# A decoder kernel's first batch: operand rows placed in two groups of eight heads, small loads behind the first, new order and bank tables

## The reference, cut to what matters

```python
x = _layernorm(x + _L0_attn_ref(x, ...))         # causal self-attention, 16 heads of 8, q and k normed
x = _layernorm(x + _L0_xattn_ref(x, ctx, ctx, ...))  # cross-attention, 16 heads of 8
x = _layernorm(x + _L0_ffn_ref(x, ...))          # 8 gated experts
x = _layernorm(x + _L1_attn_ref(x, ...))         # linear attention in chunks of 128
x = _layernorm(x + _L1_xattn_ref(x, ctx, ...))   # cross-attention, 8 heads of 128
x = _layernorm(x + _L1_ffn_ref(x, ...))          # gated feed-forward, 384 wide
```

## Time and profile before

| | us |
|---|---|
| median of 3 runs | 483.26 |
| the profiled execution, device time | 484.66 |
| its span, first to last instruction | 482.9 |
| PE busy in the span | 449.9 |
| DVE, ACT, POOL busy | 381.7, 346.9, 187.2 |
| span before the first scores (`S`) on PE | 31.97 |

### The profile page before, as it was taken

The page is one execution under the profiler, slowest core; times in us unless marked ns, Lnnn a source line. Parts: engine busy times, 40 slices in busy tenths (PEclk is TensorE's granted clock), DMA queues, the critical chain, the costliest instruction groups (busy, mean ns, idle before and its releaser), DMA issues.

```text
span 482.9 us, 14117 instructions
## 1 busy us (share of the span) xinstructions
PE 449.9 (93%) x5296; PEld 303.5 (63%) x5296; DVE 381.7 (79%) x1083; ACT 346.9 (72%) x879; POOL 187.2 (39%) x356
## 2 busy tenths in 40 slices
PE   5767889998999999999999999999999999999995
PEld 4534446654555546656778555668774765896984
DVE  2469897898899999898698988867879687764566
ACT  1635676976868878888667788996867878869642
POOL 7284000680202364434142252335334538644532
PEclk8677999999999999999999999999999999999999
DMA  7481210034200201131100000030000000000001
GB/s 230 99 209 32 76 46 5 24 89 105 60 13 14 68 2 39 39 92 34 37 4 13 13 3 4 3 76 19 3 13 14 1 1 2 1 1 1 2 12 33
DMA packets 27191, 18.50 MB, mean 38 GB/s; under 512 B 8217, under 2 KB 26773, under 8 KB 26997
## 3 DMA queue, kind: packets, MB, share of 16 engines
q1 hardware_dynamic: 23413, 15.44, 12.1%
q10 hardware_dynamic: 3712, 2.17, 1.9%
HBM read 5.58 MB, written 1.05 MB: 14 GB/s over the span
## 4 chain that ended last, share of the span: by engine, by line
PE 46%; DVE 4%; ACT 2%; POOL 1%; issue 1%; POOLq 0%; DVEq 0%; ACTq 0%
PE psum L1070 6%; PE psum L1452 6%; PE psum L1429 5%; PE psum L1463 3%; PE psum L1365 3%; PE psum L1149 2%; PE psum L1474 2%; PE psum L1176 2%; PE psum L1219 2%; PE psum L1203 2%; PE psum L1454 1%; PE psum L1321 1%; PE psum L1326 1%; PE psum L1373 1%; PE psum L1207 1%
## 5 line engine op out<-in xcount | busy, mean ns | idle before, releaser
L1600 ACT ACTIVATE EX<-psum 128x1024 f32<-128x1024 f32 (+1 forms) x128 | 119.3, 975 | 7.2 <-PE psum L1131 4.2
L1873 DVE TENSOR_REDUCE mparts<-psum 128x2 f32<-128x768 f32 (+1 forms) x96 | 77.5, 862 | 3.4 <-PE psum L1131 3.0
L1868 DVE TENSOR_REDUCE mparts<-psum 128x4 f32<-128x616 f32 (+1 forms) x80 | 68.0, 877 | 4.8 <-PE psum L1149 3.6
L1028 POOL TENSOR_TENSOR GP<-REST,xrs 128x512 f32<-128x512 f32 (+1 forms) x48 | 34.6, 743 | 48.8 <-DVE xrs L2100 24.8
L1149 PE MATMUL psum<-K,Q 64*64 64x154 bf16 (+8 forms) x1024 | 48.1, 266 | 4.9 <-DVE mparts L1873 2.2
L1176 PE MATMUL psum<-Q,K 64*64 64x512 bf16 (+7 forms) x640 | 42.9, 313 | 3.4 <-DVE mparts L1873 1.5
L1689 ACT ACTIVATE REST<-psum,nxmax 128x154 f32<-128x154 f32 x96 | 36.2, 393 | 9.2 <-DVE nxmax L2090 8.2
L1149 PEld LDWEIGHTS psum<-K,Q 64*64 64x64 bf16 x1024 | 22.3, 106 | 28.0 <-issue 14.4
L1219 PE MATMUL psum<-EX,V 128*32 128x256 f32 (+3 forms) x512 | 37.8, 435 | 1.2 <-ACT EX L1600 1.2
L954 POOL TENSOR_SCALAR rstd_rest<-moments_rest 128x2 f32<-128x2 f32 x32 | 7.3, 228 | 73.2 <-DVE moments_rest L1908 72.8
L954 POOL TENSOR_SCALAR rstd_attn<-moments_attn 128x4 f32<-128x4 f32 x8 | 1.9, 238 | 82.1 <-DVE moments_attn L1908 82.1
...
## 6 DMA issues: line engine op xcount, KB each, us to landing
...
K<-xkparts SPq DMA_DIRECT2D x24, 38.5 KB
...
Q<-in_L_xattn_Wq SPq DMA_DIRECT2D x1, 512.0 KB, 4.3
```

The lines of the kernel that those rows point to most:

```text
L1028: last = nc.gpsimd.tensor_tensor(of.XP[:, at:at + 4 * n].rearrange("p (h c) -> p h c", h=4)[:, :, 0:c1 - c0], of.XE[:, :, c0:c1], of.xrs.r ...
L1600: drains(nc.scalar.activation(dst, src, ACT.Exp), key)
L1868: last = vec.tensor_reduce(nmax[:, :, :, q], src[:, :, 0:2 * n].rearrange("p r (j k) -> p r j k", j=2), AX.X, ALU.max, negate=True)
L1873: last = vec.tensor_reduce(nmax[:, :, jj, q], src[:, :, at:at + P * (q + 1)], AX.X, ALU.max, negate=True)
```

## The change

1. Heads are laid out so that turns 0 and 1 of the first batch need partitions 0 to 63 of the parts and turns 2 and 3 the rest. Its placement is split: twelve transfers of 64 KB (`first_placed`), six on SP and six on ACT, then twelve of 64 KB on SP (`qk_placed`). The first `S` waits for the first twelve, turn 2 for the others. Batches 1 to 3 have 24 self transfers of 64 KB where they had 12 of 128 KB, all on SP.
2. Five small loads (`behind`) and the two of `eb` are issued by SP between the two groups of batch 0.
3. ACT's six `late` loads are issued after it has written q's part 0 of batch 1. POOL clears only the padding of `cT`.
4. `MERGE` and `BANK_OF` are new from the first letter to the last.

```diff
--- before.py
+++ after.py
@@ -334,31 +334,31 @@
 STREAMS = "stpfrlwcvxu0123k"
 MERGE = (
-    "rurrrruuruuruwrrrllwllurrrrrusssssuvssssutrtstsrltstssspspttttlstprssplpsttssttstlup"
...
+    "rrrrrruuuuuururlrrllwlwurrrrurusssssvsssrrsltsstttsstsspptlsttstuptssrlppwttsstststp"
...
 )
...
 BANK_OF = (
-    "565216663524627157034061302730652042614026402640246032563406204624174504264026403627"
...
+    "232403203112767305426742402761503613602460240426426013260402640624036272406026430426"
...
@@ -458,11 +458,16 @@
             return EX[:, 0, :] if w else left[:, :]
-        def placement(b, a, w, s, part):
-            n = C if a and w else S
-            to = (Q6, K6)[w][a][s:P:ROW_STEP, b % 2, :, 0:n]
-            return to, (xkparts if w else xparts)[:, part, 0:n] if a else parts[:, w, part, :]
+        def placement(b, w, s, part):
+            n = C if w else S
+            return (Q6, K6)[w][1][s:P:ROW_STEP, b % 2, :, 0:n], (
+                xkparts if w else xparts)[:, part, 0:n]
+        def half_placement(b, w, s, part, y):
+            return (Q6, K6)[w][0][s:P:ROW_STEP, b % 2, NQ * y:NQ * y + NQ, :], parts[
+                TILE * y:TILE * y + TILE, w, part, :]
...
-        def placed_until(b):
-            return 16 * (2 * SLOTS * (b + 1) + max(0, b - 1))
+        def placed_until(b, a):
+            return 16 * (2 * SLOTS * (b + 1 if a else 2 * b + 1) + max(0, b - 1))
         def parity(b, a, g):
             return TURN[b, a, g] % 2
@@ -756,22 +766,40 @@
                 (xw_raw[:, 0, :], L0_xattn_Wq), (xw_raw[:, 1, :], L0_xattn_Wk),
                 (xwv[:, :], L0_xattn_Wv), (xwo[:, :], L0_xattn_Wo),
                 (rows[:, BV:BV + 1, :].rearrange("p o d -> p (o d)"), row(L0_xattn_bv)),
-                (rows[:, BO:BO + 1, :].rearrange("p o d -> p (o d)"), row(L0_xattn_bo)),
-                (rows[:, LBO:LBO + 1, :].rearrange("p o d -> p (o d)"), row(L1_attn_bo)),
                 (col("xbq")[0:64, :], head_column(L0_xattn_bq, 0)),
                 (col("xbq")[64:P, :], head_column(L0_xattn_bq, 1)),
                 (col("xbk")[0:64, :], head_column(L0_xattn_bk, 0)),
                 (col("xbk")[64:P, :], head_column(L0_xattn_bk, 1)),
+            ]
+            behind = [
+                (rows[:, BO:BO + 1, :].rearrange("p o d -> p (o d)"), row(L0_xattn_bo)),
+                (rows[:, LBO:LBO + 1, :].rearrange("p o d -> p (o d)"), row(L1_attn_bo)),
                 (col("lbq"), column(L1_attn_bq)), (col("lbk"), column(L1_attn_bk)),
                 (col("lbv"), column(L1_attn_bv)),
             ]
-            assert len(early) == N_EARLY
-            for dst, src in early:
-                sp.dma_start(dst, src, allow_slow_non_contiguous=True).then_inc(early_loaded, 16)
+            assert len(early) + len(behind) == N_EARLY
+            def load_early(those):
+                for dst, src in those:
+                    sp.dma_start(dst, src, allow_slow_non_contiguous=True
+                                 ).then_inc(early_loaded, 16)
+            load_early(early)
             def place_self(b, y, w):
                 if b == 0 and y:
+                    if w:
+                        load_early(behind)
+                        sp.wait_ge(first_zeros_ready, 1)
+                        for m in range(2):
+                            sp.dma_start(eb[E * m:E * m + E, m, :], L0_ffn_expert_b
+                                         ).then_inc(eb_loaded, 16)
+                        for of in range(2):
+                            for s, part in (*shares(of, 0), *shares(of, 1)):
+                                sp.wait_ge(part_ready[0][part], 1 + of)
+                                sp.dma_start(*half_placement(0, of, s, part, 1)
+                                             ).then_inc(qk_placed, 16)
                     return
                 if b < 2:
                     sp.wait_ge((zeros_ready, late_zeros_ready)[b], 1 if b else 1 + w)
@@ -782,7 +810,13 @@
                 for s, part in shares(w, y):
                     sp.wait_ge(part_ready[0][part], 2 * b + 1 + w)
-                    sp.dma_start(*placement(b, 0, w, s, part)).then_inc(qk_placed, 16)
+                    if b == 0:
+                        sp.dma_start(*half_placement(0, w, s, part, 0)
+                                     ).then_inc(first_placed, 16)
+                    else:
+                        for of in HALVES:
+                            sp.dma_start(*half_placement(b, w, s, part, of)
+                                         ).then_inc(qk_placed, 16)
...
-            def wT(b, n):
-                if n == 0:
-                    sp.wait_ge(first_zeros_ready, 1)
-                    for m in range(2):
-                        sp.dma_start(eb[E * m:E * m + E, m, :], L0_ffn_expert_b
-                                     ).then_inc(eb_loaded, 16)
...
@@ -891,7 +917,7 @@
             for w, value in enumerate((0.0, TWO_ONES)):
                 nc.gpsimd.memset(words((Q6, K6)[w][0][:, 0, :, :]), value).then_inc(zeros_ready, 1)
                 pool.wait_ge(zeros_ready, w + 1)
-            step(nc.gpsimd.memset(cT[:, :, :], 0.0))
+            step(nc.gpsimd.memset(cT[:, :, C:CP], 0.0))
             nc.gpsimd.memset(eb[:, :, :], 0.0).then_inc(first_zeros_ready, 1)
             pool.wait_ge(first_zeros_ready, 1)
@@ -1137,8 +1163,10 @@
             def scores(b, a, g, u):
                 if a == b == u == g == 0:
                     pe.wait_ge(consts_ready, 1)
-                if u == g == 0:
-                    pe.wait_ge(cross_placed if a else qk_placed, placed_until(b))
+                if a == b == u == g == 0:
+                    pe.wait_ge(first_placed, 16 * 2 * SLOTS)
+                elif u == 0 and g == (0 if a or b else 2):
+                    pe.wait_ge(cross_placed if a else qk_placed, placed_until(b, a))
                 key = (b, "S", a, g, u)
                 fill(key)
                 to = pair(key)
@@ -1514,7 +1542,7 @@
                 for s, part in shares(w, y):
                     act.wait_ge(part_ready[0][part], 1 + w)
-                    act.dma_start(*placement(0, 0, w, s, part)).then_inc(qk_placed, 16)
+                    act.dma_start(*half_placement(0, w, s, part, 0)).then_inc(first_placed, 16)
             def load(those, loaded=late_loaded):
                 for dst, src in those:
                     act.dma_start(dst, src).then_inc(loaded, 16)
@@ -1540,8 +1568,6 @@
                     filled(act, (b - 1, "qkT", 1))
                     act.wait_ge(v_spread, 2 * b)
                 drains(copy(qkn[:, n, :, :].rearrange("p w d -> p (w d)"), src[:, 0:3 * D]), key)
-                if b == 1 and n == NB - 1:
-                    load(late)
             def k_norm(b):
                 if b:
@@ -1561,10 +1587,14 @@
                     act.wait_ge(bias_cols_ready, 1)
                 if b:
-                    act.wait_ge(qk_placed, placed_until(b - 1))
+                    if b == 1:
+                        act.wait_ge(first_placed, 16 * 2 * SLOTS)
+                    act.wait_ge(qk_placed, placed_until(b - 1, 0))
                 scale = col(QS) if w == 0 else col("k_scale")
                 nc.scalar.activation(parts[:, w, 0, :], src, ACT.Copy, scale=scale
                                      ).then_inc(part_ready[0][0], 1)
+                if b == 1 and w == 0:
+                    load(late)
                 if b == 0 and w:
                     for v in range(2):
                         drained(act, (0, "qkT", v))
...
...```

What the tables move, at three places. First the start on PE. `qkn` are the normed rows (`qkT`), `Q6_1` holds the per-head weights (`wT 4` and up), `X` and `Y_rest` the ctx rows (`wT 0` to `3`). Before:

```order
L1070 MATMUL psum<-ident,X 128x128 x5
L1070 MATMUL psum<-ident,Y_rest 128x26
L1060 MATMUL psum<-ident 128x128 x2
L1105 MATMUL psum<-wqkv_p,xT 128x384 x4
...
L1070 MATMUL psum<-ident,Q_1 128x128 x8
L1070 MATMUL psum<-ident,qkn 128x128 x8
L1070 MATMUL psum<-ident,X 128x128 x4
L1070 MATMUL psum<-ident,Q_1 128x128 x4
```

57 lines of the change are left out of this document (32 added, 25 removed).

## The result

The changed kernel takes 495.65 us (median of 4 runs, 494.89 to 496.14), the kernel before 483.73 beside it: ratio 1.0245, 95% interval 1.0224 to 1.0267, **11.9 us slower**. Forecast were 485.6 and a range up to 488.2. The side was right, the size was not.

A forecast was written before the change was run, and what follows sets the result against it. PE, busy 449.9 of 482.9 us, was taken as the bound, with DVE setting the early pace from 32.46. Median 483.26 plus 0 - 0.55 + 2.9 + 0 = +2.35 gave 485.6 us, range 481.6 to 488.2.

The forecast's parts named there:

- Term 1: Start up to q's part 0: earlier qkv products lose their 4.4 us waiting for per-head weights; 0, range -0.7 to +0.3.
- Term 2: First batch's placement: split transfers bring operand rows 2.1 us earlier, of which DVE's first maximum gains 0.55; -0.55.
- the rows are there at 29.8: First group's last transfer, started at about 27.5, has its rows usable 2.3 us later, 2.1 earlier than before.
- Term 3: Turns from DVE's first maximum into batch 1's turn 1: bank waits and DVE holes delay them; +2.9, bounds 1.4 to 4.3.
- the low-clock rival: Turn 0: PE's waits make PV0 run at low clock, 4.7 us for 2.36; +2.4 more, 488.0; chance 0.10.
- The holes are shorter from there, as PE is ahead in its work: After PV3: its 3.7 us delay shrinks to 2.75 at mT of batch 1's turn 1, 2.35 with one unit counted.
- The second group and the small loads: SP's issues after the first group, until 37.2, end before the maxima's transfer at about 39.2; cost 0.
- Later placements: Later batches: twelve more issues each, 7.4 us of SP, ahead of one or two maxima transfers; 0, bound +1.
- Term 4: From 80 us on: new order with the same work; 0, bounds -1.5 and +1.5, a seventh of PE's 10.6 idle us.
- Early weights: Start: per-head weights land by about 11, so the first batch moves 4.3 us forward; 481.9; chance 0.12.
- Later order pays: From 80 us on: a quarter to a half of PE's 10.6 idle us goes; -2.6 to -5, say 481.8; chance 0.16.
- No new holes: Turns 0 to 3: DVE keeps its 1.6 us of holes, leaving only the first group's gain; 482.7; chance 0.15.

The follow-up runs named there:

- e2: Kernel before with the new MERGE and BANK_OF tables throughout and nothing else: 494.33 us, ratio 1.0217.
- e14: Kernel before with the new tables for the first 51 steps only, old order behind: 488.47 us, ratio 1.0086.
- e3: Changed kernel with the new tables up to step 148 and the old ones from there: 499.29 us, ratio 1.0321.
- e8: Changed kernel with ACT's late loads back behind batch 1's last qkv copy: 494.92 us, ratio 1.0223.
- e1: Changed kernel with the MERGE and BANK_OF tables of the kernel before: 499.99 us, ratio 1.0334.
- e11: Changed kernel with the old tables and ACT's late loads back behind batch 1's last qkv copy: 495.58 us, ratio 1.0246.
- e5: Kernel before, old order, with only the twelve self placements of each later batch issued as 24 of 64 KB: 494.86 us, ratio 1.0219.
- e12: Kernel before with the new tables only from step 568 (about 280 us) on: 487.90 us, ratio 1.0068.
- e9: Changed kernel with a few dummy products in PE's waits of turns 0 and 1, to keep its clock up: 495.21 us, ratio 1.0224.
- e13: Kernel before with the new tables throughout and 24 self placements of 64 KB per later batch: 495.98 us, ratio 1.0245.
- e10: Kernel before with a few dummy products in PE's waits of turns 0 and 1 (3 ahead of the first scores): 485.79 us, ratio 1.0046.

## Why the prediction was wrong, point by point

**Term 1 (0; measured +0.8).** The mechanism was right: the wait for the per-head weights takes what the early qkv products give. But I measured it against 21.86, the latest run of all. In nine profiles with the new start q's part 0 came at 20.50 to 21.62, median 21.12; in nine with the old one at 20.11 to 21.86, median 20.30. The new start doesn't cost nothing, it costs some 0.8.

**Term 2 (-0.55).** The first maximum came at 31.84, 0.62 earlier than in the earlier trace rows, but not by halving the transfers. With transfers of 128 KB and the new order (e2) it came at 31.59. From q's part 0 to the first scores it takes 9.99 in e2 and 10.03 in e14, and with 64 KB 9.73 in the changed kernel, 9.89 in e3 and 10.31 in e8. The failed step is "the rows are there at 29.8": I had let a half transfer land 2.3 after its issue, as the small one of the maxima. The last was issued at some 27.2 and the rows were used at 31.35. Against 31.0 in an undisturbed run of the old order, the first maximum is 0.8 later.

So under the new order the rule that I weighed and set aside held. The Trainium skill, "DMA: Bandwidth & Descriptors", section Rules for kernel authors, says not to bother with two transfers to disjoint partition halves and to use one instead. By these five runs, in all of which the first scores wait for the last placement, waiting for the first half alone gains nothing either. Under the old order it gains a little: 9.80 and 9.77 in e1 and e11, for 10.24 and 10.23 in e5 and e12.

**Term 3 (+2.9, then +2.35 with one unit counted).** First maximum to `PV` of turn 0: forecast 18.25, measured 18.99, for 15.9 before. Turn 0 to turn 3: forecast 27.85, measured 28.15. Late loads: hidden, as said (e8). These steps held within 0.8; the slow `PV` is the low-clock rival come true, 1.0 of its 2.4, though in e9, without it, the end is not earlier by more than the intervals can tell. The step that failed in this term is the next one: "The holes are shorter from there, as PE is ahead in its work". From `PV` of turn 3 to `mT` of batch 1's turn 1 I let 7.0 pass for 8.0 before; it was 9.0 (87.99). Of these two us one is work that I overlooked, which the new order has ahead of this `mT`:

```profile
87.10 1.06 PE L1313 MATMUL psum<-Q,VM 128*128 128x128 f32 x8
```

Before it stood behind (82.30), so the 5.7 by which this `mT` is late overstates the lag. The next `PV` is 4.2 late (90.52 for 86.33). From `PV` to `PV` that is 11.54 for 12.07, 0.5 shorter, with 25 matmuls and 0.8 us of PE's busy time less in it: being ahead gave nothing, where I had counted 1.4.

**The second group and the small loads (0).** Right: nothing measurable between e11 and e5.

**Later placements (0, bound +1).** 1.0 under the new order (e13), not clear of noise, 11.1 under the old. The price of 7.4 us of SP's time per batch was right; "ahead of one or two transfers of maxima" was counted but never followed to who waits. It came out small only under the new order, which I did not foresee.

**Term 4 (0, ±1.5).** Measured +6.0 behind the `PV` at 90.52, 3.6 of it behind the last `PV`. This is the step on which the forecast failed. I took a seventh of the 10.6 idle us as the bound of what a new order of 700 steps could do, as if a new order could only remove or shift the idle time that is there; it can add to it. e12 shows 3.8 from the last part alone, and e2, with the order and none of the code, is 6.8 later from its `PV` at 89.30 to the end. So it is the order's doing and not the transfers'.

**The whole miss.** Against an undisturbed start the changed kernel's profile is 11.4 longer, for 2.35 in the sum. Of the 9 us between, the start is 1.4 (0.8 for -0.55), the turns up to `PV` of turn 3 are 0.8, the stretch to the next `PV` 0.9, and term 4 is 6.0. The side was right for the reason given: the turns up to turn 3 cost 5.1 us, for 4.3 forecast. But that is under half of what was measured.

**Rivals.** Early weights: false in the changed kernel (used at 16.18). Later order pays: the opposite. No new holes: false. None of them had the order cost late. The range's top of 488.2 was the low clock's; a rival "the late order loses as much as the early one" was missing; with the 6.0 measured there my sum would have been 491.6.

What stays open: which waits make the 2.7 us of the order between step 51 and 280 us, and some 0.9 of the 3.5 us of its last part. There PE is idle 1.2 more and busy 2.4 more, of which some 1.5 are steps that stood earlier in the old order; matmul ends are modelled, and no row names the rest. The slower half of e10's runs is unexplained too.
